# A graph layer with counted and gathered edges: x transposed in the loop, constant matmuls ahead of the first counts

## The reference, cut to what matters

```python
msg = x[src] + edge_attr                       # 53,125 edges, 128 features, dst sorted
neigh = segment_sum(msg, dst, 3125)
rst = (1 + eps) * x + neigh
h = rst @ W1 + b1                              # 3125 x 256
h = relu((h - mean(h, 0)) * rsqrt(var(h, 0) + 1e-5) * gamma + beta)
return layernorm(x + h @ W2 + b2)              # 3125 x 128
```

## Time and profile before

| | us |
|---|---|
| three timed runs | 289.94, 291.31, 293.26 |
| median | 291.31 |
| the profiled execution | 290.88 |
| its span | 289.1 |
| busy in the span: TensorE, VectorE, GpSimd, ScalarE | 257.7, 199.1, 195.6, 129.1 |
| mean granted TensorE clock | 0.871 |

### The profile page before, as it was taken

How to read it: one execution, slowest core, us unless ns; L and a number is a source line. 1 busy time by engine, 2 the same in 40 slices (tenths; PEclk the granted TensorE clock), 3 DMA queues, 4 the chain that set the end, 5 groups by cost and what they waited for, 6 DMA issues and landing times.

```text
span 289.1 us, 6643 instructions
## 1 busy us (share of the span) xinstructions
PE 257.7 (89%) x1995; PEld 218.9 (76%) x1995; DVE 199.1 (69%) x896; ACT 129.1 (45%) x230; POOL 195.6 (68%) x129
## 2 busy tenths in 40 slices
PE   1587799999999999999989798888989999999980
PEld 1465599998988999988868687766868888944870
DVE  3869965556556989788877687676767761178991
ACT  0456643332333555555544344344444423076594
POOL 2078888888886788888888888888888889100000
PEclk9996555555556999999999999999999999999995
DMA  6954566656665888887886777776776641000033
GB/s 174 288 148 92 120 130 145 127 139 134 128 137 112 210 194 201 189 202 165 190 206 133 165 163 164 157 149 153 174 151 145 114 72 17 2 0 0 3 107 114
DMA packets 51308, 39.14 MB, mean 135 GB/s; under 512 B 5323, under 2 KB 50299, under 8 KB 51273
## 3 DMA queue, kind: packets, MB, share of 16 engines
q1 hardware_dynamic: 32877, 30.62, 36.5%
q0 software_dynamic: 16704, 7.61, 22.1%
q10 hardware_dynamic: 1692, 0.48, 0.9%
HBM read 37.10 MB, written 1.60 MB: 134 GB/s over the span
## 4 chain that ended last, share of the span: by engine, by line
PE 55%; DMA 14%; issue 9%; DVE 8%; POOL 8%; ACT 4%; SPq 1%; DVEq 0%; ACTq 0%; POOLq 0%
PE ps L617 19%; PE ps L609 18%; POOL egat L389 8%; PE ps L638 7%; DMA egat<-in_x_dram,srci 6%; PE ps L635 5%; DMA egat<-in_edge_attr_dram 4%; DMA xN<-in_x_dram 4%; PE ps L567 4%; ACT big L504 3%; DVE xp L892 1%; DVE big L983 1%; DVE rows L884 1%; PE ps L632 1%; DVE big L985 1%
## 5 line engine op out<-in xcount | busy, mean ns | idle before, releaser
L389 POOL DMA_INDIRECT egat<-in_x_dram,srci x116 | 186.6, 1608 | 50.3 <-issue 32.5
L468 ACT ACTIVATE big<-ps 128x500 f32 x150 | 91.6, 611 | 127.3 <-PE ps L638 127.0
L609 PE MATMUL ps<-big,xp 128*128 128x114 f16 (+6 forms) x525 | 137.8, 310 | 0.0
L617 PEld LDWEIGHTS ps<-hit_c,ebuf 128*128 128x128 f32 x600 | 112.4, 219 | 10.5 <-DVE aggT L936 3.6
L617 PE MATMUL ps<-hit_c,ebuf 128*128 128x20 f32 x600 | 99.6, 256 | 3.6 <-DVE aggT L936 2.4
L609 PEld LDWEIGHTS ps<-big,xp 128*128 128x128 bf16 x525 | 87.4, 172 | 2.8
L936 DVE TENSOR_TENSOR aggT<-aggT,ps 128x20 f32 x208 | 36.0, 173 | 61.3 <-PE ps L617 55.5
L638 PE MATMUL ps<-hit_k,hit_l 128*128 128x400 f16 x150 | 57.0, 380 | 0.0
L617 PEld LDWEIGHTS ps<-hit_g,egat 128*128 128x128 f32 x232 | 42.7, 221 | 18.0 <-issue 9.4
L863 DVE TENSOR_TENSOR hit_k<-iota_k,key 128x400 f16<-128x400 f16 x150 | 54.0, 360 | 0.0
L617 PE MATMUL ps<-hit_g,egat 128*128 128x20 f32 x232 | 40.0, 262 | 10.0 <-DMA egat<-in_x_dram,srci 8.9
(11 more groups left out here) (99 smaller groups left out, 148.4 us busy)
## 6 DMA issues: line engine op xcount, KB each, us to landing
ebuf<-in_edge_attr_dram SPq DMA_DIRECT2D x75, 256.0 KB, 3.2
egat<-in_edge_attr_dram SPq DMA_DIRECT2D x57, 128.0 KB, 2.7
egat<-in_x_dram,srci POOLq DMA_INDIRECT x116, 4.0
out_dram<-big SPq DMA_DIRECT2D x6, 256.0 KB
w_sb<-in_L_gnn_W_dram ACTq DMA_DIRECT2D x2, 128.0 KB, 6.7
rows<-in_dst_dram SPq DMA_DIRECT2D x1, 192.0 KB
rows<-in_src_dram ACTq DMA_DIRECT2D x1, 192.0 KB
egat<-in_edge_attr_dram SPq DMA_DIRECT2D x1, 66.0 KB
```

Of the source, the lines that this page charges most:

```text
L389: return nc.gpsimd.indirect_dma_start(to, None, x[:, :], bass.IndirectOffsetOnAxis(ap=ix, axis=0), compute_op=op)
L468: nc.scalar.activation(cnt[:, :, bass.ds(lows[m % LOADS], WIN)], ps[:, m % BANKS_C, 0:KEYS].rearrange("p (t n) -> p t n", n=WIN), ACT.Copy ...
L609: last = nc.tensor.matmul(ps[:, ACC + f % 2, 0:SIZES[f]], xp[:, t, n, :], cnt[:, t, STARTS[f]:STARTS[f] + SIZES[f]], start=(u == 0), stop= ...
L617: last = nc.tensor.matmul(ps[:, SUMS + w % BANKS_S, 0:WIN], rows_v[:, j * D:(j + 1) * D], hits_v, start=(j == 0), stop=(j == ROWS - 1))
```

## The change

- 156 groups are counted and 52 gathered, in 9 blocks: 10, 12, 17, 25, 31, 31, 20, 8 and 2 groups, with 114, 180, 256, 376, 468, 466, 302, 120 and 110 columns a unit. The windows with units: 14 to 29 with 114 (534 columns a window), 30 to 51 with 180 (613), 52 to 85 with 256 (565), 86 to 126 with 376 (688), 127 to 167 with 468 (856), 168 to 194 with 466 (1,294), 195 to 205 with 302 (2,059), 206 and 207 with 120 (4,500). The gathered groups stand at every fourth window.
- x is transposed in the loop, three tiles in each of the windows 0 to 8 (`turn_x`), into the two banks that the blocks use later; ScalarE scales them after each of the first seven stores (`scale_x`), in an order that has the first nodes and those of the first gathered group in front. VectorE's add of a window waits for the columns it needs.
- `rest` and `part_3` run in every second window (`SPREAD`), and block 0's units wait for each part of x by itself.
- In each of the first 24 counted groups (`KEEP`) two matmuls of 400 columns on `iota_k` go into the bank of the counts and are overwritten by them.
- A counted group's order is now: half of the units, edge sum 0, a transpose, the constant matmuls and the counts of 25 and 300 columns, edge sum 1, two transposes, the counts of 400, the other half of the units.
- VectorE makes the first hits ahead of all else; the memset of spare columns of `cnt` moves to window 14. `hit_g` has two buffers instead of three; several small tiles are kept in `big` or shortened.

```diff
-GROUPS_C = 150
-BLOCKS_C = (10, 24, 30, 30, 28, 20, 8)
+GROUPS_C = 156
+BLOCKS_C = (10, 12, 17, 25, 31, 31, 20, 8, 2)
...
+SPREAD = 2
+X_RATE = 3
+LATE = 14
+BATCHES_G = 2
+KEEP = 24
...
+        def columns_of(g):
+
+            return max(0, nominal(g) - MARGIN) // BANK, min(N - 1, nominal(g) + MARGIN + WIN) // BANK
+
+        early_g = columns_of(GC)[0]
+        X_ORDER = [0] + [b for i in range(NB) for b in (early_g + i, 1 + i) if (b < NB if b >= early_g else b == 1 + i)]
+        X_ORDER = list(dict.fromkeys(X_ORDER))
+        X_TILES = [(i, t) for i, b in enumerate(X_ORDER) for t in range(*pieces(b))]
...
+            def scale_x(i):
+
+                b = X_ORDER[i]
+                act.wait_ge(x_turned, i + 1)
+                nc.scalar.activation(aggT[:, b * BANK:b * BANK + width(b)], ps[:, ACC + i % 2, 0:width(b)], ACT.Copy,
+                                     scale=b2e[:, D:D + 1]).then_inc(x_scaled, 1)
...
-                act.wait_ge(spare_zeroed, 1)
...
+                    if m == GC - LATE:
+                        act.wait_ge(spare_zeroed, 1)
...
-                        t0, t1 = pieces(m)
+                        scale_x(m)
+                    if m % SPREAD == SPREAD // 2 - 1 and m // SPREAD < NB:
+                        b = m // SPREAD
+                        t0, t1 = pieces(b)
                         nc.scalar.activation(xp[:, t0:t1, 0, :], upper(xN[:, t0:t1, :]), ACT.Copy).then_inc(x_first_made, 1)
-                        act.wait_ge(x_rest_made, m + 1)
-                        nc.scalar.activation(xp[:, t0:t1, 1, :], upper(xr[:, m % 2, 0:t1 - t0, :]),
+                        act.wait_ge(x_rest_made, b + 1)
+                        nc.scalar.activation(xp[:, t0:t1, 1, :], upper(xr[:, b % 2, 0:t1 - t0, :]),
                                              ACT.Copy).then_inc(x_middle_made, 1)
...
-            pe.wait_ge(x_loaded, 32)
-            for b in range(NB):
-                if b >= 2:
-                    pe.wait_ge(x_scaled, b - 1)
-                t0, t1 = pieces(b)
-                for t in range(t0, t1):
+            def turn_x(n0, n1):
+
+                for n in range(n0, min(n1, NT)):
+                    i, t = X_TILES[n]
+                    t0, t1 = pieces(X_ORDER[i])
                     r = rows_of(t)
                     k = (t - t0) * P
-                    last = nc.tensor.transpose(ps[:, b % 2, k:k + r], xN[0:r, t, :], ident[0:r, 0:r])
-                last.then_inc(x_turned, 1)
+                    if n == 0:
+                        pe.wait_ge(x_loaded, 32)
+                    if t == t0 and i >= 2:
+                        pe.wait_ge(x_scaled, i - 1)
+                    last = nc.tensor.transpose(ps[:, ACC + i % 2, k:k + r], xN[0:r, t, :], ident[0:r, 0:r])
+                    if t == t1 - 1:
+                        last.then_inc(x_turned, 1)
...
+                        if f == 0 and u % (4 * PARTS) == 0:
+                            pe.wait_ge(x_first_made, t // 4 + 1)
+                            pe.wait_ge(x_middle_made, t // 4 + 1)
+                            pe.wait_ge(x_last_made, t // 4 + 1)
                         if u == 0:
                             pe.wait_ge(counts_stored, ENDS[f])
-                            if f == 0:
-                                pe.wait_ge(x_first_made, NB)
-                                pe.wait_ge(x_middle_made, NB)
-                                pe.wait_ge(x_last_made, NB)
+                            if f < 2:
+                                pe.wait_ge(x_scaled, NB)
...
+                def counts_a(m):
+
                     pe.wait_ge(key_hits_made, m + 1)
                     if m >= BANKS_C:
                         pe.wait_ge(counts_stored, m - BANKS_C + 1)
+                    if m < KEEP:
+                        for n in range(2):
+                            nc.tensor.matmul(ps[:, m % BANKS_C, 0:KEYS_B], iota_k[:, 0:P], iota_k[:, 0:KEYS_B], start=True,
+                                             stop=True, skip_group_check=True)
                     if m > 0:
                         if (m - 1) % CARRY == 0:
                             pe.wait_ge(carry_hits_made, (m - 1) // CARRY + 1)
-                        nc.tensor.matmul(o[:, :, 0], hit_l[:, (m - 1) % RING_K, 1, :],
+                        nc.tensor.matmul(counted(m)[:, :, 0], hit_l[:, (m - 1) % RING_K, 1, :],
                                          hit_n[:, (m - 1) // CARRY % 2, (m - 1) % CARRY, :], start=True, stop=False,
                                          skip_group_check=True)
-                    nc.tensor.matmul(o[:, :, 0:WIN_A], hit_l[:, r, 0, :],
-                                     hit_k[:, r, 0:KEYS_A].rearrange("p (t n) -> p t n", n=WIN_A), start=(m == 0),
-                                     stop=False, skip_group_check=True)
-                    nc.tensor.matmul(o[:, :, FROM_B:WIN], hit_l[:, r, 1, :],
-                                     hit_k[:, r, KEYS_A:KEYS_A + KEYS_B].rearrange("p (t n) -> p t n", n=WIN_B),
+                    nc.tensor.matmul(counted(m)[:, :, 0:WIN_A], hit_l[:, m % RING_K, 0, :],
+                                     hit_k[:, m % RING_K, 0:KEYS_A].rearrange("p (t n) -> p t n", n=WIN_A),
+                                     start=(m == 0), stop=False, skip_group_check=True)
+
+                def counts_b(m):
...
-                    ua, ub = u0 + (u1 - u0) // 3, u0 + 2 * (u1 - u0) // 3
+                    ua = u0 + (u1 - u0 + 1) // 2
...
                     edge_sum(w, 0, rows_v, hits[:, h, :])
-                    multiply(f, ua, ub)
+                    turn_x(X_RATE * w, X_RATE * w + 1)
+                    if w in C_OF:
+                        counts_a(C_OF[w])
+                    else:
+                        multiply(f, ua, u1)
                     edge_sum(w, 1, rows_v, hits[:, h + 1, :])
-                    multiply(f, ub, u1)
+                    turn_x(X_RATE * w + 1, X_RATE * (w + 1))
                     if w in C_OF:
-                        counts(C_OF[w])
+                        counts_b(C_OF[w])
+                        multiply(f, ua, u1)
                 multiply(F - 1, 0, UNITS)
                 pe.wait_ge(counts_stored, GC)
                 hidden(0, EARLY * HH)
...
-                dve.wait_ge(carry_turned, 1)
-                dve.wait_ge(lo_turned, 1)
-                nc.vector.memset(cnt[:, :, CNT - SPARE:CNT], 0.0).then_inc(spare_zeroed, 1)
                 dve.wait_ge(constants_made, 7)
+                dve.wait_ge(lo_made, 1)
+                hits_k(0)
                 hits_c(0)
+                hits_k(1)
+                hits_n(0)
+                hits_k(2)
                 hits_g(0)
-                dve.wait_ge(lo_made, 1)
-                for m in range(AHEAD):
-                    hits_k(m)
-                hits_n(0)
                 dve.wait_ge(x_loaded, 32)
-                dve.wait_ge(x_scaled, NB)
                 dve.wait_ge(src_rows_made, 1)
...
+                        b0, b1 = columns_of(g)
+                        if v < 4 * NB or b0 != b1:
+                            dve.wait_ge(x_scaled, max(X_ORDER.index(b) for b in range(b0, b1 + 1)) + 1)
...
-                    if w < NB:
-                        rest(w)
-                    if 1 <= w <= NB:
-                        part_3(w - 1)
+                    if w % SPREAD == 1 and w // SPREAD < NB:
+                        rest(w // SPREAD)
+                        part_3(w // SPREAD)
+                    if w == SPREAD * NB:
+                        dve.wait_ge(lo_turned, 1)
+                        dve.wait_ge(src_turned, 1)
+                        nc.vector.memset(cnt[:, :, CNT - SPARE:CNT], 0.0).then_inc(spare_zeroed, 1)
```

More of the change, by code:

```diff
@@ L134, in gnn_layer @@
         dcol = part(T)
+        src_all = part(T).bitcast(I32)
         rl = part(2 * BANK).rearrange("p (a n) -> p a n", a=2)
+        bst = part(HH * NB * 6).rearrange("p (h b s) -> p h b s", h=HH, b=NB)
+        lst = part(NT * 6).rearrange("p (t s) -> p t s", s=6)
+        lag = part(NT * 2).rearrange("p (t s) -> p t s", s=2)
+        lsd, lrs, lnb = (part(NT) for _ in range(3))
         at[0] = 0
@@ L370, in _ @@
             nc.gpsimd.memset(xN[:, NT - 1, :], 0.0).then_inc(x_padded, 1)
-            nc.gpsimd.iota(diff[:, :], [[1, P]], base=0, channel_multiplier=-1,
+            nc.gpsimd.iota(ident[:, :], [[1, P]], base=0, channel_multiplier=-1,
                            allow_small_or_imprecise_dtypes=True).then_inc(constants_made, 1)
@@ L620, in edge_sum, with counted @@
                         last.then_inc(window_summed, 1)
-                def counts(m):
-                    r = m % RING_K
-                    o = ps[:, m % BANKS_C, 0:KEYS].rearrange("p (t n) -> p t n", n=WIN)
+                def counted(m):
+                    return ps[:, m % BANKS_C, 0:KEYS].rearrange("p (t n) -> p t n", n=WIN)
+                def counts_a(m):
                     pe.wait_ge(key_hits_made, m + 1)
@@ L654, in _ @@
                         rows_v = egat[:, k, :]
```

(9 more changed lines are left out.)

52 lines of the change are left out of this document (25 added, 27 removed).

## The result

| | median us | runs | ratio to the kernel before, 95% interval |
|---|---|---|---|
| before | 290.62 | 289.55 to 293.26 | |
| changed | 280.62 | 278.88 to 281.48 | 0.9635 (0.9552 to 0.9718) |

The row "before" has a fourth run, 289.55, beside the three of the table ahead. Executions more than 1.5% above the fastest of their kernel are left out of the ratios, but not of the medians.

A forecast was written before the change was run, and what follows sets the result against it. Gathers were taken to bound the loop to window 168 (181.0 us), then TensorE: 50.8 to the last add, 4.9 last pass, 36.4 tail, 273.1 of span, plus 1.8 beside it: 275 us, range 266 to 288.

The forecast's parts named there:

- What bounds the kernel: Main loop: GpSimd's gathers, 58 groups at 3.87 us, set the pace to about 202 us, then TensorE to 246.
- The gathers' term: Loop up to window 168: 52 gathered groups at 3.83 us, plus 8.6 us to the add, put it at 181.0.
- TensorE's slack: Loop up to window 168: TensorE alone arrives at about 171, gathers allow 181; 10 us hide dummies, transposes and block changes.
- Will the clock rise: Early loop: TensorE's granted clock goes to 2.4 GHz by about 30 us, under the constant matmuls and transposes.
- Rival (a): Early loop: constant matmuls don't lift the clock, the multiplies do at window 32; 291 us, no change; chance 0.10.
- The end: After window 168: 50.8 us to the last add at 231.8, last pass 4.9 at 0.065 a unit, tail 36.4.
- Rival (d): TensorE's last 40 windows: stalls from blocks and banks, or repeated clock dips, cost 5 to 10 us; 283 us; chance 0.15.
- The sum: Whole span: last add 231.8 plus last pass 4.9 plus tail 36.4 gives 273.1 us.

The follow-up runs named there:

- Experiment 5: Changed kernel with the old grouping (150 counted, 58 gathered, seven old blocks): six runs at 289.67 to 291.73 us, six at 296.94 to 300.17.
- Experiment 3: Changed kernel without the two constant matmuls (KEEP = 0): 281.55 us.
- experiment 4: Kernel before with only the constant matmuls added ahead of the counts of the first 24 counted groups: 288.48 us, ratio 0.9941.
- experiment 6: Changed kernel with x transposed ahead of the loop again, constant matmuls kept: 281.50 us.
- experiment 1: Changed kernel with GpSimd's add of b2 to x waiting until VectorE's last key hits: 274.38 us, ratio 0.9455.
- experiment 8: Experiment 1's kernel (late GpSimd add) with x transposed ahead of the loop and without the constant matmuls: 274.36 us.
- experiment 10: Experiment 1's kernel with the 52 gathered windows sparser at the start and denser at the end: 267.50 us, ratio 0.9213.
- experiment 2: Changed kernel with GpSimd's add of b2 to x cut into 25 instructions at its old place: 282.07 us in two runs.
- experiment 7: Experiment 1's kernel (late GpSimd add) without the constant matmuls (KEEP = 0): 277.02 us.

## Why the prediction was right, and where it was off

**What bounds the kernel: right.** Experiment 5 takes back the regrouping alone and the gain goes with it, with TensorE idle for 20.9 us on gathers' DMAs; experiments 3, 4 and 6 show that clock and start hardly count. 52 gathered groups instead of 58 are what pays.

**The gathers' term: 4.3 us too small.** I had window 168 at 181.0; it is at 185.3. Three us are the second issue of 4.46 us, which the kernel before doesn't have (it took 1.66 at the same place). The rest is the 3.83 that I took a group: between groups 1 and 41 of the changed kernel it is (176.79 - 22.06) / 40 = 3.87, and 41 x 0.04 = 1.6. Leaving the waits out was right, as the changed kernel has none over 0.31 us; but its issues are each a little longer, 1.63 us in the mean without the second, against 1.61 before. Why isn't shown. The way from issue to add, 8.6 us, came out at 8.5.

**TensorE's slack: right.** The model said 10 us; experiment 1 shows 9.1 us of waits for gathers, and experiment 8 uses all but 1.7 of it up without losing time. Window 32 I had at 58; it is at 58.3. (The first edge sum, at 16.2 us, is 1 us earlier than forecast.)

**Will the clock rise: right.** It rose at 21 us, after the first two windows. Experiment 3 shows that the constant matmuls were needed, as the transposes in the loop didn't hold it. They lift it but don't guarantee it: with them, it was at 1.2 GHz once more from 33.3 to 43.6 us in experiment 6 and from 34.4 to 41.3 in experiment 10. Rival (a), that the constant matmuls don't lift the clock, was seen in no run. Its course, a rise only under the multiplies, is what experiments 3 and 8 did (near 70 us) by leaving the constant matmuls out. I had priced it at 291 with window 32 at 83, and 24 x 0.67 = 16 of that are the constant matmuls' own time; without them the same sum gives 67, and the two experiments have 68.8 and 66.7.

**The end: near enough, but for one event.** From the add of window 168 to that of window 207 experiment 1, which has no stall, takes 233.1 - 185.5 = 47.6 us. I had 50.8. 1.1 us of this is a slip: I counted 27 + 11 + 2 = 40 windows where 39 lie between the two adds. The units of 110 and 120 columns are cheaper than my 0.065 us, as the end of the changed kernel shows; the last pass of 75 takes 3.6:

```profile
236.31 2.10 PE L641 MATMUL ps<-big,xp 128*128 128x120 f16 x37
238.25 0.35 PE L649 MATMUL ps<-hit_g,egat 128*128 128x20 f32 x2
239.64 3.79 PE L641 MATMUL ps<-big,xp 128*128 128x110 f16 x75
243.27 1.94 PE L595 MATMUL ps<-aggT,w_sb 128*128 128x512 f32 x4
```

The distance is 0.048 to 0.052 us a unit, near the low bound of columns / 2,400. The other two of the 3.2 us that were too many lie in the 26 windows of 1,294 columns (1.04 us each instead of 1.09, 1.3 in all) and in the 13 windows behind them (0.8). The 81 ns that the Trainium skill gives for such pairs (TensorE: Matmul & The Clock Gate, Back-to-back issue gap) does not hold here. The tail from 243.27 is 36.4, as forecast.

**The step that was missed.** I followed the gathers to their end and stopped there. Behind them on GpSimd stands the add of b2 to x, 7.56 us, which in the kernel before began 1.6 us after VectorE's last compare had ended. With the gathers ending 20 us earlier it falls into the loop. What the faster engine would trigger next stood in the timeline of GpSimd, and I did not ask. The Trainium skill has the rule (GPSIMD Engine Reference, 1. Specifications): GpSimd's way to SBUF is shared with VectorE, with contention for VectorE instructions with two SBUF inputs. The traces here agree: a compare with two SBUF inputs takes 7.95 us in the changed kernel and 10.37 in experiment 2, while in the kernel before adds with one input in PSUM take their 0.17 to 0.18 beside the same GpSimd add. It cost 3.7 us of idle TensorE and, as an estimate, about 3 us through the low clock after it (6.9 us between the last adds of the changed kernel and of experiment 1, less 3.7); experiment 1 gave back 6.2. Rival (d) had foreseen stalls and a dip of the clock in the last 40 windows, 5 to 10 us, but laid them to the blocks and their banks. The size and the place came, the cause was another.

**The sum.** 4.3 us from the gathers and 7.1 from the stall (54.63 us from window 168 to 207 against 47.55), less 3.2 in these windows otherwise and 1.6 in the last pass (3.3 against 4.9): 6.6 us over 273.1. That the miss is no larger is in part luck: 11.4 us were missing from the sum, and 4.8 too much elsewhere in it hid a part of them.

## What to carry to other kernels

When a change shortens an engine's work, write down the next instruction of that engine too, with its new time, and look what the other engines do just then: here a 7.5 us GpSimd add, harmless where it stood, held VectorE as soon as it came 20 us earlier. Find the chain that paces the loop before paying for the others: a doubled clock for 50 us gave nothing while gathers set the pace, and 5.7 us when they no longer did. Where two chains run side by side at different speeds, spacing the coupled work after the speed of each stage (experiment 10) brought 7 us for a few lines.

## What the runs showed of the hardware that I had not expected

- A VectorE compare of 256 fp16 elements with both inputs in SBUF took 7.95 us beside one GpSimd tensor_tensor of 7.55 us, and 10.37 us beside the same work in 25 instructions. It was held, not slowed in proportion. VectorE's adds with one input in PSUM took 0.17 to 0.18 us beside the same GpSimd add (kernel before, 239.17 to 246.20).
- The reverse may hold too, but isn't proven: a GpSimd gather issue took 4.46 to 4.8 us instead of 1.6 under a gapless stream of VectorE compares, and 2.46 when the stream ended earlier; the issue ahead of it took 1.7 under the same stream.
- The stall's second bill came from the clock: after 3.72 us of idle TensorE the granted clock was 1.2 GHz from 226 to about 232 us.
- The length of the gap ahead of it doesn't tell when the clock falls. A gap of 1.85 us from 131.7 was followed by 6.8 us at 1.2 GHz. In the kernel before a gap of 1.95 us was followed by no fall (first line below).
- Transposes ahead of the loop lifted the clock in the kernel before (the matmul of 300 columns took 0.29 us right behind all 25), but not in every execution: in experiment 6, with the same 25 ahead, it took 0.43 at 25.07 us (second line below). Three in each of the first nine windows didn't hold it (experiments 3 and 7).

```profile
163.61 0.37 PE L617 MATMUL ps<-hit_g,egat 128*128 128x20 f32 x2 [1.95 <-DMA egat<-in_x_dram,srci]
...
25.07 0.43 PE L670 MATMUL ps<-hit_k,hit_l 128*128 128x300 f16 x1
```
